# Token transposes as 64 rows by 64 columns on two row halves of TensorE's array, with other banks and an earlier place for the dt transposes

## The chip, the cores and the metric

One core of one Trainium2 chip runs the whole program. The metric is the device time of one execution in microseconds (us), the median of several runs. A profiled execution of the same program gives the trace.

## What is computed

Three steps on x (64 sequences of 32 tokens of 512 channels), all in float32. A conditional mixing of channels gives the input of a Mamba-2 block with 64 heads of 64 channels, 8 groups of 8 heads and a state of 128. Its output is added to x. Then a grouped convolution, a dense layer with a cluster mask, and a second addition.

```python
proj = jnp.einsum('bld,pd->blp', hidden_states, in_proj_w)
xBC  = silu(conv(proj[x, B, C]))            # 4 taps over the tokens
dt_p = softplus(dt + dt_bias);  dA = exp(dt_p * A)
dtx  = dt_p[..., None] * x                  # per token and head
state = state * dA_t + dtx_t * B_t;  y_t = state . C_t     # over 32 tokens
y = y + x * D
yn = y * rsqrt(mean(y*y per group) + eps) * norm_weight * silu(gate)
x = x + yn @ out_proj_w.T
x = x + masked(conv2(x) @ weight.T + bias)
```

## The kernel before

The Mamba part is 32 stages, `stage(n)`: a half of the tokens, one of the 8 groups of heads, and a block of 512 tokens (four tiles of 128). A stage has ten slots, m = 0 to 9. In slot m TensorE makes one 128 x 512 slice of the projection, `proj(n, m)` (line 487), as twelve matmuls in rounded float32: slots 0 and 1 are B and C, slots 2 to 5 the four slices of x, 6 to 9 those of the gate. The recurrence over 32 tokens is done as matrix products: G = B.C (`G_all`, line 621), the decays as exp of a product `seg` (lines 579 and 580) made by ScalarE (`expo`, line 588, tile Lt), M = decay times G on VectorE (`M_dve`, line 650, tile big), and `Y` (line 670), 64 by 64 products of dtx with M.

For dtx the slices of x, which lie with channels in the partitions, have to be turned so that tokens do. `A(n, i)` (line 610) does it for token tile i: four transposes of 128 x 128 with a 128 column identity as the moving operand, into one PSUM bank. Tiles 0 and 1 are turned at the end of slot 7, tiles 2 and 3 at the end of slot 9, right ahead of `Y(n, 0)` and `Y(n, 1)`. `A_dve` (line 641) multiplies a turned tile by dt out of PSUM. Tiles 2 and 3 are used in the next stage's slots 0 to 2, where `Y(n, 2)`, `Y(n, 3)` run. The output products `O(n - 1, i)` (line 770) of the stage before run in slots 1, 3, 4 and 5, each followed by its small sums `S` (line 738).

All five engines work in order, and the order is written out by hand: each `op` goes to its engine's queue where the Python code reaches it, each `wait` stops that engine alone until a named event. PSUM has eight banks: PP three for the projection in turn, PG for G and sums, PY two for Y, PO one for each output product, SEG two for the decays, and PT. TB lists the banks that the four token tiles are turned into: (PT, PO[2], PT, PO[0]). PO[0] is also SEG[0], so tile 3 waits until ScalarE has read the first decays, `L(n, 0)`; tile 2 waits for `dtx(n, 0)`, which frees PT.

Four times in the run a new block of dt values is made: `D_pe` (line 385) in slot 8 of stages 15, 16 and 0 (and at the start), then a chain of thirteen steps, `D_chain`, mostly on VectorE (lines 418 to 436, the last one `dsp` at line 427), of which the tuples `pace0` (stage 0) and `pace` (others) say how many are put ahead of each slot's work. `DT_pe` (line 444) turns the results, waiting for `dsp`; `DT_split` has ScalarE and VectorE copy them; `av` (line 560) has GpSimd make the operands of `seg` from the copies. In stages 0, 1, 16 and 17 (`turned_now`) these three stand in slot 6 behind `proj(n, 6)`; `seg(n)` follows in slot 8.

After stage 31 come `last_products` and the second part, which the change meets only through other bank numbers.

Of the kernel before, what the change touches and what calls it, by code (L numbers as in the profile page):

```python
# [56 lines left out]
def adaln_attn_ffn_kernel(nc, x, emb, gin, b2, wbank, biask, w_in, w_dt, w_out, prm, cst, cw4, ctxw,  # L57
                          w_ffn, b_ffn, asg, x2s, out):
    ctx = ExitStack()
    with ctx:  # L60
        def sb(name, shape, dt=F32):
            return ctx.enter_context(nc.sbuf_tensor(name, shape, dt))

        acc = sb("acc", [128, NT, XP])
        xh = sb("xh", [128, 4, 1024], FR)
        xl = sb("xl", [128, 4, 1024], FR)
# [15 lines left out]
        dtt = sb("dtt", [128, 8, 64])  # L82
# [6 lines left out]
        xs = big[:, 0:2048].rearrange("p (j t) -> p j t", j=4)  # L89
# [5 lines left out]
        dtx = sb("dtx", [128, 2, 512])  # L95
# [23 lines left out]
        pmx = gmt[:, 2, :]  # L119
        ex = gmt[:, 0:2, :]  # L120
        PS = ctx.enter_context(nc.psum_tensor("PS", [128, 8, 512], F32))
        PP, PT, PG, PY, PO = (0, 1, 4), 2, 3, (5, 6), (7, 7, 5, 6)
        SEG = (7, 6)
        TB = (PT, PO[2], PT, PO[0])

        book = {}
        pe, act, dve, pool, sp = (Queue(book) for _ in range(5))
        ident = C[:, C_ID:C_ID + 128]
# [4 lines left out]
        def bc(a, *shape):  # L133
            return a.to_broadcast(list(shape))
# [240 lines left out]
        def D_pe(b, free):  # L375
            a = 512 * (b % 2)
            pe.wait("wd", 0)
            pe.wait("wdl", 0)
            pe.wait("xl", 4 * b + 3)
            for w in free:  # L380
                pe.wait(*w)
            n = 0
            for k in range(4):
                for w, v in ((wdh, xh), (wdh, xl), (wdl, xh)):
                    fn = lambda e, k=k, w=w, v=v, n=n: e.matmul(PS[0:64, D_bank(b), :], w[:, 64 * k:64 * k + 64],
                                                                v[:, k, a:a + 512], start=(n == 0), stop=(n == 11))
                    pe.op(fn, "D", b) if n == 11 else pe.op(fn)
                    n += 1
# [50 lines left out]
        def DT_pe(b, free):  # L439
            pe.wait("dsp", b)  # L440
            for w in free:
                pe.wait(*w)
            for i, src in enumerate((dr[:, 0:128], dr[:, 128:256], da[:, 0:128], da[:, 128:256])):
                fn = lambda e, i=i, src=src: e.transpose(PS[:, SEG[0], 128 * i:128 * i + 128], src, ident)
                pe.op(fn, "DT", b) if i == 3 else pe.op(fn)

        def DT_split(b):
            a = 4 * (b % 2)
            turned = lambda t: t[:, a:a + 4, :].rearrange("p (r i) c -> p i r c", r=2)
            dt, av_ = (PS[:, SEG[0], k:k + 256].rearrange("p (i r c) -> p i r c", i=2, r=2) for k in (0, 256))  # L450
            act.wait("DT", b)
            act.op(lambda e: e.copy(turned(dtt), dt), "dtt", b)
            act.op(lambda e: e.copy(turned(ah), av_), "ah", b)
            dve.wait("ah", b)
            dve.op(lambda e: e.tensor_tensor(turned(al), av_, f(turned(ah)), ALU.subtract), "alo", b)
# [95 lines left out]
        def av(n):  # L551
            half, g, tb = who(n)
            b = 2 * half + tb
            pool.wait("dtt", b)
            pool.wait("ah", b)
            pool.wait("alo", b)
            if n >= 1:
                pool.wait("O", (n - 1, 3))
            for src, dst, kind in ((ah, avh, "avh"), (al, avl, "avl")):
                pool.op(lambda e, src=src, dst=dst: e.tensor_tensor(  # L560
                    dst.rearrange("p (i h t) -> p i h t", i=4, h=8),
                    bc(f(src[:, 4 * tb:4 * tb + 4, 8 * g:8 * g + 8]).rearrange("p i (h o) -> p i h o", o=1), 128, 4, 8, 32),
                    bc(C[:, C_V:C_V + 32].rearrange("p (a b t) -> p a b t", a=1, b=1), 128, 4, 8, 32), ALU.mult), kind, n)

        def seg(n):
            pe.wait("avh", n)
            pe.wait("avl", n)
            pe.wait("uf", 1)
            if n == 0:
                pe.wait("alo", 0)  # L570
            for r in range(2):
                if r == 0 and n - 1 in block_at:
                    pe.wait("ah", block_at[n - 1])
                    pe.wait("alo", block_at[n - 1])
                if n >= 1:
                    pe.wait("acc", (n - 1, 1 + 2 * r))
                else:
                    pe.wait("xl", 5 + r)
                pe.op(lambda e, r=r: e.matmul(PS[:, SEG[r], :], uf[:, :], avh[:, 512 * r:512 * r + 512], start=True, stop=False))
                pe.op(lambda e, r=r: e.matmul(PS[:, SEG[r], :], uf[:, :], avl[:, 512 * r:512 * r + 512], start=False, stop=True),  # L580
                      "seg", (n, r))
# [5 lines left out]
                    act.wait("M", (n - 1, 3))  # L587
                act.op(lambda e, r=r: e.activation(Lt[:, 512 * r:512 * r + 512], PS[:, SEG[r], :], ACT.Exp), "L", (n, r))  # L588

        def A(n, i):  # L590
            a = 128 * i
            if i == 2 and n in block_at:
                pe.wait("dre", (block_at[n], 1))
            if i == 0:
                if n == 0:
                    pe.wait("dre", (0, 1))
                elif n in block_at:
                    pe.wait("xl", 4 * block_at[n] + 3)
                for m in range(6):
                    pe.wait("silu", (n, m))  # L600
                if n >= 1:
                    pe.wait("dtx", (n - 1, 2))
            elif i == 1:
                pe.wait(*(("acc", (n - 1, 2)) if n >= 1 else ("xl", 7)))
            elif i == 2:
                pe.wait("dtx", (n, 0))
            else:
                pe.wait("L", (n, 0))
            for j in range(4):
                fn = lambda e, j=j: e.transpose(PS[:, TB[i], 128 * j:128 * j + 128], xs[:, j, a:a + 128], ident)  # L610
                pe.op(fn, "T", (n, i)) if j == 3 else pe.op(fn)

        def G_all(n):
            pe.wait("silu", (n, 0))
# [19 lines left out]
        def A_dve(n, i):  # L634
            half, g, tb = who(n)
            z, r = 4 * n + i, i % 2
            dve.wait("T", (n, i))
            dve.wait("dtt", 2 * half + tb)
            if z >= 2:
                dve.wait("Y", divmod(z - 2, 4))  # L640
            dve.op(lambda e: e.tensor_tensor(  # L641
                dtx[:, r, :].rearrange("p (h c) -> p h c", h=8), PS[:, TB[i], :].rearrange("p (h c) -> p h c", h=8),
                bc(dtt[:, 4 * tb + i, 8 * g:8 * g + 8].rearrange("p (h o) -> p h o", o=1), 128, 8, 64), ALU.mult), "dtx", (n, i))
        def M_dve(n, i):
            r = i % 2
            if i >= 2 or n >= 1:
# [85 lines left out]
        def S(n, tiles):  # L732
            last = (n, tiles[-1])
            pe.wait("ys2", last)
            pe.wait(*shared[0])
            shared[0] = ("var", last)
            for i in tiles:
                fn = lambda e, i=i: e.matmul(PS[:, PG, 256 + i:257 + i], yss[:, i, :], C[:, C_ONE:C_ONE + 1], start=True, stop=True)
                pe.op(fn, "S", last) if i == tiles[-1] else pe.op(fn)
# [72 lines left out]
        mixing_weights_pool(1)  # L812
        decay_rates()

        pace0 = (0, 3, 2, 3, 2, 3, 0, 0, 0, 3)
        pace = (0, 0, 0, 0, 5, 5, 0, 0, 0, 3)
        block_at = {0: 1, 15: 2, 16: 3}

        def X_tile(T, n):
# [7 lines left out]
        chain = []  # L827

        def stage(n):
            prev = n >= 1  # L830
            b = block_at.get(n)
            if n == 0:
                chain.extend(D_chain(0))
            for m in range(10):
# [31 lines left out]
                        add_out(n - 1, i)  # L866
                if m == 3 and not prev:
                    G_mask(n)
                turned_now = n == 0 or n - 1 in block_at
                if m == 6 and not turned_now:  # L870
                    av(n)
                if n == 0 and m == 6:
                    side_inputs()
# [13 lines left out]
                if m == 2:  # L887
                    silu(n, 1)
                evac(n, m)
                if m == 6 and turned_now:  # L890
                    t = block_at[n - 1] if n else 0
                    assert not chain
                    DT_pe(t, [("acc", (n - 1, 1)) if n else ("xl", 5)])
                    DT_split(t)
                    av(n)
                if n == 0 and m < 6:
                    split_w_hi(0, m + 4)
                    split_w_lo(0, m + 4)
# [32 lines left out]
                if prev:  # L931
                    for i in at("O"):
                        O(n - 1, i)
                        for tiles in sums(n - 1):
                            if tiles[-1] == i:
                                S(n - 1, tiles)
                if m == 7:
                    A(n, 0)
                    A(n, 1)
                if m == 8:  # L940
                    seg(n)
                    expo(n)
                    if b is not None:
                        D_pe(b, [("dtx", (n, 0))])
                        chain.extend(D_chain(b))
                if m == 9:
                    A(n, 2)
                    A(n, 3)
                    Y(n, 0)
                    Y(n, 1)  # L950

# [138 lines left out]

        FB = ((SEG[0], PP[2]), PY)

# [298 lines left out]
```

How the kernel before makes its waits and increments, by code:

```python
    def emit(self, eng, sems):  # L43
        seen = {}
        for it in self.items:
            if it[0] == "wait":
                v = self.book[it[1]][it[2]]
                if seen.get(it[1], 0) < v:
                    eng.wait_ge(sems[it[1]], v)
                    seen[it[1]] = v
            else:
                ins = it[1](eng)
                if it[2] is not None:
                    ins.then_inc(sems[it[2]], it[3])
```

## Time and profile before

| | |
|---|---|
| median of 3 runs | 1626.84 us (1625.94 to 1626.89) |
| the profiled execution | 1627.06 us, of which the span from first to last instruction 1625.3 us |
| TensorE matmuls busy | 1604.8 us, 99% of the span |
| weight loads | 1299.1 us, 80% |
| VectorE, ScalarE, GpSimd busy | 65%, 52%, 48% |
| mean granted TensorE clock | 0.998 |
| line 610 (token transposes) | 512 transposes, 272 ns each |

A matmul's time runs from its start until its last result is out, and the next one starts before that, so the busy time adds up to more than what an instruction costs the queue. What it costs is the distance from its start to the next one's start. In the timeline a row is a start, a duration over all merged instructions, an engine (PE is TensorE's matmuls, PEld its weight loads), a line, the tiles written and read (written<-moving,stationary in alphabetical order), the tile of the array (rows*columns), the moving operand's shape, and a count; in brackets is idle time before it and what ended it.

### The profile page before, as it was taken

What the parts mean: (1) busy time and instruction counts of PE and PEld (TensorE: products, weight loads), DVE (VectorE), ACT (ScalarE), POOL (GpSimd) and SP (SyncE); (2) the same over time, 40 slices, a digit from 0 to 9 for tenths busy, and PEclk for the clock granted to TensorE, in tenths of its full rate; (3) what the DMA queues carried; (4) which work ended last, traced back from release to release, by engine and by line L of the source; (5) the groups of instructions that cost most, each with busy time, mean ns of one, the idle gap of its engine ahead of it and who ended that gap; (6) DMA issues with size and microseconds to landing.
All of it is one profiled execution on the core that took longest, in us unless ns stands there. A gap on an engine that the chain in (4) does not pass through costs nothing. (4 is left out here: it accounts for less than half of the span.)

```text
span 1625.3 us, 31516 instructions
## 1 busy us (share of the span) xinstructions
PE 1604.8 (99%) x12495; PEld 1299.1 (80%) x12495; DVE 1059.1 (65%) x1741; ACT 845.9 (52%) x1372; POOL 773.4 (48%) x731
## 2 busy tenths in 40 slices
PE   9999999999999999999999999999999999999997
PEld 6778888888888888887787888888888888887665
DVE  6876666565656576676686656565667656565455
ACT  4654546555555545565554555555555556544321
POOL 3564644545453645454255554646364545534203
PEclk9999999999999999999999999999999999999999
DMA  5111102011111101011112201111110201116772
GB/s 190 59 53 33 41 20 66 27 53 40 40 53 34 59 16 58 21 53 40 33 41 73 65 28 53 41 40 53 34 59 8 66 21 53 41 36 153 181 156 104
DMA packets 50290, 93.08 MB, mean 57 GB/s; under 512 B 5664, under 2 KB 6304, under 8 KB 50144
## 3 DMA queue, kind: packets, MB, share of 16 engines
q1 hardware_dynamic: 50144, 91.06, 19.6%
q8 instruction: 100, 1.64, 0.4%
q14 instruction: 46, 0.38, 0.1%
HBM read 82.59 MB, written 8.45 MB: 56 GB/s over the span
## 5 line engine op out<-in xcount | busy, mean ns | idle before, releaser
L487 PE MATMUL PS<-xh,wh 128*128 128x512 f32 x1280 | 518.7, 405 | 0.6 <-DVE xl L369 0.6
L487 PE MATMUL PS<-xh,wl 128*128 128x512 f32 x1280 | 500.0, 391 | 0.0
L487 PE MATMUL PS<-xl,wh 128*128 128x512 f32 x1280 | 499.8, 390 | 0.0
L522 DVE SCALAR_TENSOR_TENSOR cb<-PS,P,cb 128x496 f32<-128x496 f32 (+2 forms) x576 | 412.6, 716 | 132.5 <-ACT cb L508 119.0
L184 POOL TENSOR_TENSOR wl<-rw,wh 128x512 fp32r<-128x512 f32 x160 | 211.8, 1328 | 188.6 <-ACT wh L179 170.6
L721 POOL TENSOR_TENSOR ysum<-yq 128x256 f32<-128x256 f32 x128 | 109.4, 855 | 364.0 <-ACT yq L706 363.8
L487 PEld LDWEIGHTS PS<-xh,wl 128*128 128x128 f32 x1280 | 240.2, 188 | 52.9
L487 PEld LDWEIGHTS PS<-xh,wh 128*128 128x128 f32 x1280 | 240.5, 188 | 49.1 <-ACT wh L179 1.0
L487 PEld LDWEIGHTS PS<-xl,wh 128*128 128x128 f32 x1280 | 241.0, 188 | 44.3
L508 ACT ACTIVATE cb<-PS,P 128x512 f32<-128x512 f32 x192 | 148.4, 773 | 205.2 <-PE PS L487 205.2
L650 DVE TENSOR_TENSOR big<-Lt,gmt 128x512 f32<-128x512 f32 x128 | 102.6, 843 | 158.0 <-ACT Lt L588 158.0
L770 PE MATMUL PS<-oh,yh 128*128 128x512 f32 x512 | 200.0, 391 | 2.4 <-POOL yl L730 2.4
L770 PE MATMUL PS<-ol,yh 128*128 128x512 f32 x512 | 199.2, 389 | 0.0
L770 PE MATMUL PS<-oh,yl 128*128 128x512 f32 x512 | 199.2, 389 | 0.0
L706 ACT ACTIVATE yq<-y 128x512 f32<-128x512 f32 x128 | 81.0, 633 | 207.0 <-DVE y L687 200.7
L512 ACT ACTIVATE big<-PS 128x512 f32<-128x512 f32 x128 | 76.2, 595 | 149.0 <-PE PS L487 148.7
L542 ACT ACTIVATE big<-cb 128x512 f32<-128x512 f32 x192 | 119.5, 623 | 62.7 <-DVE cb L522 62.5
L783 DVE SCALAR_TENSOR_TENSOR acc<-PS,rs,acc 128x512 f32<-128x512 f32 x128 | 93.1, 749 | 84.0 <-issue 45.9
L751 POOL TENSOR_TENSOR rs<-vr,mh 128x1 f32<-128x1 f32 (+1 forms) x95 | 57.0, 600 | 166.6 <-DVE vr L746 166.4
L641 DVE TENSOR_TENSOR dtx<-PS,dtt 128x512 f32<-128x512 f32 x128 | 82.1, 683 | 56.8 <-PE PS L610 56.8
L770 PEld LDWEIGHTS PS<-oh,yh 128*128 128x128 f32 x512 | 96.1, 188 | 23.0 <-issue 3.4
L770 PEld LDWEIGHTS PS<-oh,yl 128*128 128x128 f32 x512 | 96.1, 188 | 20.0
(197 smaller groups left out, 2230.6 us busy)
## 6 DMA issues: line engine op xcount, KB each, us to landing
rw<-in_w_in SPq DMA_DIRECT2D x160, 256.0 KB, 2.7
ro<-in_w_out SPq DMA_DIRECT2D x64, 256.0 KB, 2.9
wh<-x2s SPq DMA_DIRECT2D x32, 258.5 KB, 5.2
wl<-x2s SPq DMA_DIRECT2D x32, 258.5 KB, 5.1
x2s<-acc SPq DMA_DIRECT2D x16, 260.0 KB, 5.5
out_x<-acc SPq DMA_DIRECT2D x16, 256.0 KB, 2.3
acc<-in_x SPq DMA_DIRECT2D x3, 1024.0 KB, 9.4
acc<-in_x SPq DMA_DIRECT2D x4, 256.0 KB, 4.8
```

What stands on the lines that cost most here:

```text
L184: pool.op(lambda e: e.tensor_tensor(wl[:, m, :], rw[:, q % RW, :], f(wh[:, m, :]), ALU.subtract), "w_lo", (u, m))
L487: fn = lambda e, k=k, w=w, v=v, i=i: e.matmul(PS[:, bank, :], w[:, m, 128 * k:128 * k + 128], v[:, k, a:a + 512], start=(i == 0), stop=(i ...
L508: act.op(lambda e: e.activation(cb[:, z % 2, :], PS[:, bank, :], ACT.Identity, bias=P[:, P_CB + c:P_CB + c + 1], scale=P[:, P_CW + 4 * c + ...
L512: act.op(lambda e: e.activation(gate[:, m - 6, :], PS[:, bank, :], ACT.Silu), "ev", (n, m))
L522: dve.op(lambda e, d=d, w=w: e.scalar_tensor_tensor(out=cv[:, :, d:32], in0=pv[:, :, 0:32 - d], scalar=w, in1=cv[:, :, d:32], op0=ALU.mult ...
L542: act.op(lambda e: e.activation(dst, cb[:, z % 2, :], ACT.Silu), "silu", (n, m))
L641: dve.op(lambda e: e.tensor_tensor(dtx[:, r, :].rearrange("p (h c) -> p h c", h=8), PS[:, TB[i], :].rearrange("p (h c) -> p h c", h=8), bc ...
L650: dve.op(lambda e: e.tensor_tensor(Mb[:, r], bc(Lt[:, 256 * i:256 * i + 256].rearrange("p (h o t) -> p h o t", h=8, o=1), 128, 8, 2, 32), ...
L706: act.op(lambda e: e.activation(yq[:, :], y[:, r, :], ACT.Square), "yq", (n, i))
L721: pool.op(lambda e: e.tensor_tensor(ysum[:, :], yq[:, 0:256], yq[:, 256:512], ALU.add), "ys1", (n, i))
L770: fn = lambda e, j=j, v=v, w=w, q=q: e.matmul(PS[:, O_bank(n, i), :], v[:, r, 128 * j:128 * j + 128], w[:, j, :], start=(q == 0), stop=(q ...
L783: dve.op(lambda e: e.scalar_tensor_tensor(out=acc[:, T, 4:516], in0=PS[:, O_bank(n, i), :], scalar=rs[:, i:i + 1], in1=acc[:, T, 4:516], o ...
```

## The change

The token transposes become 64 by 64: `A(n, r)` now turns a pair of token tiles with sixteen instructions in place of eight. Each takes 64 partitions of xs (one row half, v = 0 or 1) with 128 token columns as the stationary operand and a 64 x 64 piece of the identity as the moving one, and writes 64 columns into the bank of its half. The pair of tiles shares the two banks. `A_dve` reads its tile out of both banks, and waits for the pair's one event. Banks are renumbered so that each pair is adjacent: PP (0, 1, 2), PT 6, PY (4, 5), PO (7, 7, 5, 4), SEG (7, 4). The waits move with it: the first pair waits for `dtx(n - 1, 3)` and `acc(n - 1, 2)` at its start, the second for `dtx(n, 1)` and `L(n, 0)` at its start. `D_pe` waits for `dtx(n, 1)`. In stages 1, 16 and 17 `DT_pe` and `DT_split` move from behind `proj(n, 6)` to the end of slot 5, behind `O(n - 1, 3)` and its sums; `av` goes to the head of slot 6. The chain's pace changes from 5 and 5 steps in slots 4 and 5 to 7 and 3, in stage 0 from 3, 2, 3, 2, 3 in slots 1 to 5 to 3, 3, 3, 3, 1.

```diff
-        PP, PT, PG, PY, PO = (0, 1, 4), 2, 3, (5, 6), (7, 7, 5, 6)
-        SEG = (7, 6)
-        TB = (PT, PO[2], PT, PO[0])
+        PP, PT, PG, PY, PO = (0, 1, 2), 6, 3, (4, 5), (7, 7, 5, 4)
+        SEG = (7, 4)
+        TB = ((PO[2], PT), (PT, PO[0]))
...
-                    pe.wait("xl", 5 + r)
+                    pe.wait("xl", 5 + 2 * r)
...
-        def A(n, i):
...
-            for j in range(4):
-                fn = lambda e, j=j: e.transpose(PS[:, TB[i], 128 * j:128 * j + 128], xs[:, j, a:a + 128], ident)
-                pe.op(fn, "T", (n, i)) if j == 3 else pe.op(fn)
+        def A(n, r):
+            if r == 0:
+                for m in range(6):
+                    pe.wait("silu", (n, m))
+                if n == 0:
+                    pe.wait("dre", (0, 1))
+                    pe.wait("xl", 7)
+                else:
+                    pe.wait("dtx", (n - 1, 3))
+                    pe.wait("acc", (n - 1, 2))
+                if n in block_at and n >= 1:
+                    pe.wait("xl", 4 * block_at[n] + 3)
             else:
+                pe.wait("dtx", (n, 1))
                 pe.wait("L", (n, 0))
+                if n in block_at:
+                    pe.wait("dre", (block_at[n], 1))
+            for i in (0, 1):
+                a = 128 * (2 * r + i)
+                for j in range(4):
+                    for v in (0, 1):
+                        p, c = slice(64 * v, 64 * v + 64), 256 * i + 64 * j
+                        fn = lambda e, j=j, v=v, a=a, p=p, c=c: e.transpose(PS[:, TB[r][v], c:c + 64], xs[p, j, a:a + 128],
+                                                                         ident[p, 64 * v:64 * v + 64])
+                        pe.op(fn, "T", (n, 2 * r + 1)) if (i, j, v) == (1, 3, 1) else pe.op(fn)
...
+            b0 = TB[i // 2][0]
+            dve.wait("T", (n, i | 1))
...
+                dtx[:, r, :].rearrange("p (j v c) -> p j v c", j=4, v=2),
+                PS[:, b0:b0 + 2, 256 * r:256 * r + 256].rearrange("p v (j c) -> p j v c", j=4),
...
-        pace0 = (0, 3, 2, 3, 2, 3, 0, 0, 0, 3)
-        pace = (0, 0, 0, 0, 5, 5, 0, 0, 0, 3)
+        pace0 = (0, 3, 3, 3, 3, 1, 0, 0, 0, 3)
+        pace = (0, 0, 0, 0, 7, 3, 0, 0, 0, 3)
...
-                turned_now = n == 0 or n - 1 in block_at
-                if m == 6 and not turned_now:
+                if n >= 1 and m == 6:
                     av(n)
...
-                if m == 6 and turned_now:
-                    t = block_at[n - 1] if n else 0
+                if n == 0 and m == 6:
                     assert not chain
-                    DT_pe(t, [("acc", (n - 1, 1)) if n else ("xl", 5)])
-                    DT_split(t)
-                    av(n)
+                    DT_pe(0, [("xl", 5)])
+                    DT_split(0)
+                    av(0)
...
+                if n - 1 in block_at and m == 5:
+                    assert not chain
+                    DT_pe(block_at[n - 1], [("acc", (n - 1, 1))])
+                    DT_split(block_at[n - 1])
                 if m == 7:
                     A(n, 0)
-                    A(n, 1)
...
-                        D_pe(b, [("dtx", (n, 0))])
+                        D_pe(b, [("dtx", (n, 1))])
...
                 if m == 9:
-                    A(n, 2)
-                    A(n, 3)
+                    A(n, 1)
```

## Rows read from the trace of the kernel before

**Rows 1.** The page, part 1: busy time, share of the span, instructions.
```profile
PE 1604.8 (99%) x12495; PEld 1299.1 (80%) x12495; DVE 1059.1 (65%) x1741; ACT 845.9 (52%) x1372; POOL 773.4 (48%) x731
```

**Rows 2.** Timeline of TensorE, stage 15, first group of transposes (start, us, engine, ...).
```profile
747.62 1.03 PE L610 MATMUL PS<-C,big 128*128 128x128 f32 x8
748.41 0.48 PE L487 MATMUL PS<-xh,wh 128*128 128x512 f32 x1
748.72 0.39 PE L487 MATMUL PS<-xl,wh 128*128 128x512 f32 x1
748.95 0.40 PE L487 MATMUL PS<-xh,wl 128*128 128x512 f32 x1
```

**Rows 3.** TensorE's groups by shape (busy us, mean ns), then durations min/median/max by line.
```profile
L610 PEld LDWEIGHTS PS<-C,big 128*128 128x128 f32 x512 | 59.7, 140 | 8.3
L738 PEld LDWEIGHTS PS<-C,big 128*128 128x128 f32 x256 | 43.0, 189 | 7.4
...
L610 PE MATMUL PS<-C,big x512: 270/272/273, 58.6 to 1491.2; 128*128 128x128 f32 x171
...
L670 PE MATMUL PS<-big,dtx x4096: 218/218/268, 71.5 to 1500.0; 64*64 64x64 f32 x196
```

**Rows 4.** Timeline of TensorE, stage 15: from 128 rows to 64, and one Y.
```profile
716.14 0.39 PE L487 MATMUL PS<-xh,wl 128*128 128x512 f32 x1
716.46 0.49 PE L355 MATMUL PS<-ab,xb 64*128 64x512 f32 x1
...
718.21 1.16 PE L670 MATMUL PS<-big,dtx 64*64 64x64 f32 x64
719.30 0.46 PE L621 MATMUL PS<-big 128*32 128x32 f32 x32
```

**Rows 5.** Timeline of TensorE, stage 14, second group, Y, next projection.
```profile
702.81 1.03 PE L610 MATMUL PS<-C,big 128*128 128x128 f32 x8
703.88 1.30 PE L670 MATMUL PS<-big,dtx 64*64 64x64 f32 x64
705.11 0.50 PE L487 MATMUL PS<-xh,wh 128*128 128x512 f32 x1
705.45 0.40 PE L487 MATMUL PS<-xl,wh 128*128 128x512 f32 x1
```

**Rows 6.** Timeline of ScalarE and VectorE beside rows 5; what line 670 waited for.
```profile
699.37 0.60 ACT L512 ACTIVATE big<-PS 128x512 f32<-128x512 f32 x1 [1.68 <-PE PS L487]
...
702.51 1.09 ACT L588 ACTIVATE Lt<-PS 128x512 f32<-128x512 f32 x2
...
703.13 1.29 DVE L650 TENSOR_TENSOR big<-Lt,gmt 128x512 f32<-128x512 f32 x2 [4.20 <-ACT Lt L588]
...
  DVE big L650: 6.1, 26
```

**Rows 7.** Timeline of VectorE and TensorE in stage 0, around the second group.
```profile
67.55 1.29 DVE L650 TENSOR_TENSOR big<-Lt,gmt 128x512 f32<-128x512 f32 x2 [3.10 <-ACT Lt L588]
...
70.52 1.03 PE L610 MATMUL PS<-C,big 128*128 128x128 f32 x8
```

**Rows 8.** Timeline of TensorE and VectorE in stage 17, the dt transposes.
```profile
844.75 0.48 PE L487 MATMUL PS<-xh,wh 128*128 128x512 f32 x1
...
848.12 0.44 PE L444 MATMUL PS<-C,dr 128*128 128x128 f32 x2 [0.37 <-DVE da L427]
...
856.47 0.47 PE L579 MATMUL PS<-yh,uf 128*128 128x512 f32 x1 [1.34 <-issue]
...
836.26 1.35 DVE L430 TENSOR_TENSOR da<-pb,dr 128x256 f32<-128x256 f32 x1
```

**Rows 9.** Timeline of TensorE in stage 1, the same place.
```profile
102.53 0.48 PE L487 MATMUL PS<-xh,wh 128*128 128x512 f32 x1
...
105.89 0.44 PE L444 MATMUL PS<-C,dr 128*128 128x128 f32 x2 [0.38 <-DVE da L427]
...
113.97 0.47 PE L579 MATMUL PS<-yh,uf 128*128 128x512 f32 x1 [1.05 <-issue]
```

More of the change, by code:

```diff
@@ L588, in expo @@
                 act.op(lambda e, r=r: e.activation(Lt[:, 512 * r:512 * r + 512], PS[:, SEG[r], :], ACT.Exp), "L", (n, r))
-        def A(n, i):
[L591 to L594, printed above, removed]
+        def A(n, r):
+            if r == 0:
+                for m in range(6):
+                    pe.wait("silu", (n, m))
                 if n == 0:
                     pe.wait("dre", (0, 1))
-                elif n in block_at:
-                    pe.wait("xl", 4 * block_at[n] + 3)
[L599 to L606, printed above, removed]
+                    pe.wait("xl", 7)
[3 more added lines that the diff above has]
+                if n in block_at and n >= 1:
+                    pe.wait("xl", 4 * block_at[n] + 3)
             else:
+                pe.wait("dtx", (n, 1))
                 pe.wait("L", (n, 0))
-            for j in range(4):
-                fn = lambda e, j=j: e.transpose(PS[:, TB[i], 128 * j:128 * j + 128], xs[:, j, a:a + 128], ident)
-                pe.op(fn, "T", (n, i)) if j == 3 else pe.op(fn)
+                if n in block_at:
[8 more added lines that the diff above has]
+                        pe.op(fn, "T", (n, 2 * r + 1)) if (i, j, v) == (1, 3, 1) else pe.op(fn)
         def G_all(n):
@@ L636, in A_dve @@
             z, r = 4 * n + i, i % 2
-            dve.wait("T", (n, i))
+            b0 = TB[i // 2][0]
+            dve.wait("T", (n, i | 1))
             dve.wait("dtt", 2 * half + tb)
@@ L641, in A_dve @@
             dve.op(lambda e: e.tensor_tensor(
-                dtx[:, r, :].rearrange("p (h c) -> p h c", h=8), PS[:, TB[i], :].rearrange("p (h c) -> p h c", h=8),
-                bc(dtt[:, 4 * tb + i, 8 * g:8 * g + 8].rearrange("p (h o) -> p h o", o=1), 128, 8, 64), ALU.mult), "dtx", (n, i))
+                dtx[:, r, :].rearrange("p (j v c) -> p j v c", j=4, v=2),
+                PS[:, b0:b0 + 2, 256 * r:256 * r + 256].rearrange("p v (j c) -> p j v c", j=4),
+                bc(dtt[:, 4 * tb + i, 8 * g:8 * g + 8].rearrange("p (j v o) -> p j v o", j=4, v=2), 128, 4, 2, 64), ALU.mult), "dtx", (n, i))
         def M_dve(n, i):
```

## The prediction

> **What bounds the kernel now.** I read the page first, then TensorE's own timeline stage by stage, and only then the other engines at the places where TensorE stood still. The page has TensorE's matmuls busy 99% of the span [rows 1], and no other engine above 65%. So the time is the sum of the distances from one matmul's start to the next one's, and a change on another engine counts only where TensorE waits for it. Outside such waits the timeline is very regular: a 128x512 matmul is followed by the next after 0.23 us (the last two rows of [rows 2]), and the distances repeat from stage to stage. Every cost below is such a distance. The reader should look at the starts, not at the durations.
>
> Two places matter. In slot 7 the first group of eight transposes stands between two projections, and nothing waits: it costs 0.79 us (747.62 to 748.41), and the projection behind it comes up to speed late, 0.31 us to its second matmul in place of 0.23 [rows 2], about 0.11 us with what follows. So the first group costs 0.90 us. In slot 9 the second group stands ahead of Y. There the starts are 702.81 and 703.88 [rows 5], but I don't read that as the price of the transposes, because Y also waits for M: ScalarE's two exps start at 702.51 and take 1.09, so the first ends near 703.1; VectorE starts the first M at 703.13, two take 1.29 [rows 6], so the first M ends near 703.8, and Y starts just after it. Line 670 is released by M 26 times [rows 6].
>
> **The price of a new transpose.** The eight old ones start 0.109 us apart (a round). Why decides what halving brings. A token transpose has a weight load of 140 ns; another float32 load of 128 columns takes 189 [rows 3]. So the transposes' load is some 50 ns shorter, and the load alone doesn't fill 109 ns. The matmul with 128 moving columns takes 272 ns, that of Y with 64 takes 218 [rows 3]: 54 ns for 64 columns, 108 for 128. That is the round: the moving columns bound it and the load hides behind them. With 64 moving columns it is 54, and the load of 128 columns (109 less 50, some 58) about equals it. So a row half does one transpose per 58 ns or so, if the load stays as short.
>
> Whether both halves work at once is shown by Y alone. One Y pair is 64 instructions on four 64*64 tiles with one bank for each row half, the same split. It takes 1.09 us to the next line [rows 4] = 16 rounds of four. Taking 0.11 for the first round (load, then columns) and 0.15 for the drain before the next tile shape, the other fourteen rounds come to 0.83/14 = 0.059 us. Row halves and column halves run together there. I take 0.059 for a round of two new transposes; the other end is 0.059 for each transpose alone, and 0.11 a round if the load turns long.
>
> **The price of the switch.** Rows 4 show the same tile shape, 64*128, entered from the projection: 716.14 to 716.46 is 0.32 us in place of 0.23, so 0.09 for the drain. Leaving 64 rows costs more: the last round drains (0.15), and the next projection needs 0.34 us to its second matmul (705.11 to 705.45 [rows 5]), 0.11 over the usual and some 0.02 more behind it. Old transposes had no entry and little exit cost, as they have the projection's own shape. The Trainium skill, TensorEngine Tiling, section Key Properties, says that changing the tiling mode drains TensorE; the rows above agree and give its size.
>
> **First group, 32 stages.** New: entry 0.09, first round 0.11, six rounds of 0.059 = 0.35, the drain 0.15 and a few ns for the second half, exit 0.13: 0.84 us. Old 0.90. So 0.06 a stage, 32 times = 1.9 us saved. The transposes themselves fall from 0.87 to 0.46; the two switches take nearly all of it back. All of what follows on the other engines moves along: ScalarE idles 1.68 us until the projection of slot 8 is done (699.37 [rows 6]), so it is driven by TensorE here and gives the gain through.
>
> **Second group, 27 ordinary stages.** The chain that sets Y's start runs from the end of projection 8 over ScalarE (silu, skip product, weight split, table load, exps) to the first M, and doesn't contain the transposes. It stays. The new group waits for the first L at its start (near 703.1, 0.3 us after TensorE gets there), then takes 0.11 + 0.35 + 0.15 = 0.61: done near 703.77, some 0.1 ahead of Y's old start at 703.88. Zero gained, zero lost, with M as the cover; were that cover gone, the gain would be 0.26 a stage. The second half of Y waits for the second M (Y takes 1.23 here, 1.09 where M is early [rows 4, 5]), so an earlier start would bring nothing either.
>
> **Second group, stages with M early.** In stage 0 both M are done by 68.84 and the group starts at 70.52 [rows 7]. There the old group costs 8 x 0.109 + 0.1 = 0.97 to Y, the new one 0.09 + 0.61 = 0.70. Stages 0, 15, 16 (a dt product stands behind seg) and 31 are such: 4 x 0.26 = 1.0 us saved.
>
> **dt transposes, stages 1 and 17.** Moving them ahead of projection 6 pays only if the chain's last step is done by then. In stage 17 TensorE gets to projection 6 at 844.75. The dt transposes ran at 848.12, released by line 427, the chain's end [rows 8], after a stall of 0.5 behind the projection (whose twelve matmuls fill 2.83). In the new order TensorE stands at the wait from 844.75: 3.3 us with nothing to do, and projection 6 is behind it. The new pace moves two steps from slot 5 to slot 4, ahead of the taps there; but VectorE works without idling from 836.26 [rows 8] to slot 5, so its total ahead of the last step is the same, and I move that end by at most 0.2. What goes is the old stall 0.5 and the wait of seg for av on GpSimd (1.34 before 856.47 by the profile, 1.5 as distance): seg now comes after the work of GpSimd. Net 3.3 - 2.0 = 1.3 later. Stage 1 in the same way: 102.53 to 105.89, 3.3 us; gone are 0.5 and 1.2 (1.05 before 113.97) [rows 9]: 1.6 later. With the stall gone before seg, these two become ordinary and Y waits for M again: 0.14 each. In stage 16 the chain ends before TensorE reaches even the new place: 0. In stage 0 the place stays, VectorE is full ahead of it, and the reshuffled pace brings 0 (bounds -0.5 and +0.5). Sum +3.2 us. The bounds for the two stages are 0 stall left (then both stalls go: -3.7) and 1 us more each.
>
> **The rest at nothing.** Bank numbers change no instruction. `A_dve` reads two banks with the same 512 elements; Y's reader on VectorE has that pattern already, and dtx is needed three slots later. `dtx(n, 0)` may start up to 0.4 us later, with over 5 us until slot 9. The new waits of `A(n, 0)` are for events two slots old. `D_pe` waits for dtx(n, 1), done long before.
>
> **Sum.** -1.9 - 1.0 + 3.2 = +0.3 us on the profiled 1627.06; that execution is 0.2 above the median, so 1626.84 + 0.3 = 1627.1 us.
>
> **The rivals.** (1) The chain ends in time: VectorE gets through the seven steps while it would otherwise wait for slot 4's data, and the stalls of stages 1 and 17 vanish. Then -3.7 in place of +3.2 (with up to half of it more likely than all): 1620 to 1624. For it: seven steps are put where the taps wait for ScalarE. Against: rows 8 show no such idle time. (2) The switch is cheaper for the transposes than for line 355 and Y, as both are in float32 and leave no long column stream: drains nearly vanish, first group 0.55, so 32 x 0.3 = 10 more: 1617. Against: rows 4 and 5. The Trainium skill, TensorEngine Tiling, section Theoretical Speedup, gives up to 2x for 64 rows; for both groups that would be half of 64 x 0.87, 28 us, which the wait for M in slot 9 alone rules out. (3) Slower by a long load: with 64 rows the transposes' load loses its short form and takes 109 ns like the others of 128 columns. A round stays at 0.11, sixteen instructions do the old work, and the switches come on top. First group 0.09 + 0.94 + 0.13 = 1.16, +0.26 x 32 = 8.3; second group past M's time by 0.2 to 0.25, of which Y's own wait gives 0.14 back, +0.08 x 27 = 2.2, and 0.3 for the others; with dt +3.2: +14, 1641. It decides from a round of about 0.07 on. The Trainium skill, TensorE: Matmul & The Clock Gate, section LDWEIGHTS, has the load go by its columns alone, 107 ns for 128: by that rule this rival would hold; the 140 against 189 ns in rows 3 speak against it. (4) The halves take turns: 16 x 0.059, first group 1.29, +12; second group +6.5; with dt +22: 1649. Against it: Y's rounds. (5) My drains are off by 0.05: inside the forecast's own range.
>
> **Chances.** The forecast (within 1624 to 1630) 0.50; rival 1 0.16; rival 2 0.06; rival 3 0.10; rival 4 0.06; other slower ways, as the second group ending behind M by 0.1 to 0.2 us, 0.12 (1630 to 1635). The range takes in rival 1 and rival 3 and leaves out 2 and 4: 1620 to 1641. A measurement of this kernel tells 0.2%, 3.3 us, from no change. Faster 0.22, same 0.50, slower 0.28. The forecast's own range is 1624 to 1630.
>
> **What would show it.** Right: in slot 7 the group and what follows at 0.7 and 0.1 us, rounds of 59 ns, weight loads of 140 ns, 0.32 us entry; in slot 9 Y still released by line 650 with Y's start 1.0 to 1.1 after the end of projection 9; idle time of some 3 us before line 444's successor in stages 1 and 17 and none before line 579 there. Wrong: loads of 188 ns (rival 3), starts 59 ns apart one by one (rival 4), no stall before the dt transposes (rival 1), a next projection that starts within 0.1 us of the last transpose (rival 2).

## The result, and the profile after

The changed kernel takes 1629.66 us (median of 20 runs, 1627.28 to 1631.98) against 1626.87 us of the kernel before, run beside it. The ratio is 1.0015, interval 1.0009 to 1.0022: 2.8 us more. That is a small slowdown clear of noise, inside the 0.2% that was taken as no change (the interval ends just above it). The profiled execution took 1628.14 us, its span 1626.4 us, only 1.1 us over the span before. That gap between the profile and the median is a finding of its own, below.

The page, part 1 (busy us, share of the span, instructions), and what TensorE waited for (us in total, times, longest), of the changed kernel:

```profile
PE 1595.7 (98%) x13007; PEld 1278.0 (79%) x13007; DVE 1056.9 (65%) x1741; ACT 845.3 (52%) x1372; POOL 774.1 (48%) x731
...
PE PS L444 <- DVE da L427: 6.7, 3, 3.2
PE PS L612 <- ACT Lt L588: 6.5, 28, 0.3
PE PS L775 <- POOL yl L735: 2.4, 2, 1.5
...
PE PS L579 <- issue: 1.7, 1, 1.7
```

TensorE is 9 us less busy than in [rows 1], and waits more: 6.7 us for the end of the dt chain, and 28 times for the first exp (line 588) at the head of the second group. Of the waits before `seg` (line 579) only that of stage 0 is left. In the kernel before, the same two waits were:

```profile
PE PS L579 <- issue: 4.1, 3, 1.7
...
PE PS L444 <- DVE da L427: 1.6, 3, 0.8
```

The first group of transposes, now line 612, timeline of TensorE in stage 13, and the line's durations (min/median/max):

```profile
650.28 0.39 PE L487 MATMUL PS<-xh,wl 128*128 128x512 f32 x1
650.60 0.71 PE L612 MATMUL PS<-C,big 64*128 64x64 f32 x16
651.25 0.50 PE L487 MATMUL PS<-xh,wh 128*128 128x512 f32 x1
651.58 0.39 PE L487 MATMUL PS<-xl,wh 128*128 128x512 f32 x1
...
L612 PEld LDWEIGHTS PS<-C,big x1024: 134/139/143, 57.9 to 1492.2; 64*128 64x128 f32 x171
L612 PE MATMUL PS<-C,big x1024: 221/222/278, 57.9 to 1492.3; 64*128 64x64 f32 x171
```

Entry 0.32 us in place of 0.23, sixteen transposes and the drain 0.64 (640 to 644 ns in each of the 32 stages, where the old eight took 790), then 0.33 to the second matmul of the projection. With 0.02 to 0.03 behind it that is 0.09 + 0.64 + 0.13 = 0.86, against 0.90 in [rows 2]. The load still takes 139 ns and the matmul has fallen by 50 to 222; the reading of [rows 3] was 54.

The second group in stage 13, all engines (compare [rows 5, 6]):

```profile
657.33 1.09 ACT L588 ACTIVATE Lt<-PS 128x512 f32<-128x512 f32 x2
...
657.95 1.29 DVE L655 TENSOR_TENSOR big<-Lt,gmt 128x512 f32<-128x512 f32 x2 [5.31 <-ACT Lt L588]
658.04 0.61 PEld L612 LDWEIGHTS PS<-C,big 64*128 64x128 f32 x16 [0.57 <-issue]
658.07 0.71 PE L612 MATMUL PS<-C,big 64*128 64x64 f32 x16 [0.18 <-ACT Lt L588]
...
658.71 1.29 PE L675 MATMUL PS<-big,dtx 64*64 64x64 f32 x64
...
659.93 0.19 PEld L487 LDWEIGHTS PS<-xh,wh 128*128 128x128 f32 x1
```

The transposes stand and wait for the exp, and Y follows 0.64 us after their start, when both the group and the first M (which ends near 658.65) are through. Those 0.64 us are what the first group takes, where nothing is waited for: so in 28 stages the transposes now stand in the chain themselves, between the exp and Y, and end when M does. From the start of the exps to Y it is 1.38 us, and it was 1.37 in [rows 5, 6] (702.51 to 703.88). Y's start came out 0.01 us later and Y itself 0.01 shorter. Nothing came back here.

The dt transposes in stages 1 and 17, TensorE's timeline, and the granted clock (PEclk, 1.00 is 2.4 GHz) of two stretches:

```profile
101.35 0.28 PE L743 MATMUL PS<-C,big 128*128 128x1 f32 x2
104.83 0.44 PE L444 MATMUL PS<-C,dr 128*128 128x128 f32 x2 [3.21 <-DVE da L427]
...
110.87 0.71 PE L612 MATMUL PS<-C,big 64*128 64x64 f32 x16
...
843.80 0.28 PE L743 MATMUL PS<-C,big 128*128 128x1 f32 x2
847.26 0.69 PE L444 MATMUL PS<-C,dr 128*128 128x128 f32 x2 [3.19 <-DVE da L427]
...
849.03 0.63 PE L487 MATMUL PS<-xh,wl 128*128 128x512 f32 x1
849.46 0.63 PE L487 MATMUL PS<-xh,wh 128*128 128x512 f32 x1
...
854.83 0.71 PE L612 MATMUL PS<-C,big 64*128 64x64 f32 x16
...
104.00:106.00 2.00, 1.17 (x7) 1.06 (x8) 1.93 (x4) 0.48 (x2) 0.00 (x0) 1.00 0.44 131
846.00:850.00 4.00, 2.74 (x9) 2.35 (x10) 3.52 (x8) 0.65 (x2) 0.20 (x2) 0.63 0.25 70
...
848.00:850.00 2.00, 2.00 (x7) 1.61 (x6) 1.70 (x4) 0.65 (x2) 0.19 (x1) 0.50 0.06 23
```

Both stalls are 3.2 us. Behind the one in stage 17 the matmuls start 0.43 us apart in place of 0.23 and last 0.63 in place of 0.39: the granted clock, the third figure from the right, is 0.50 there, its lower level, 1.2 GHz (0.63 is the mean of a stretch with both levels). From the dt transposes to the first group it is 6.04 us in stage 1 (104.83 to 110.87) and 7.57 in stage 17 (847.26 to 854.83): the lower clock costs 1.5 us. In this execution it happened once. Of the 20 timed runs, the four with a mean granted clock of 0.998 took 1627.3 to 1628.2 us, the two with 0.993 took 1631.7 and 1632.0, most of the others were at 0.996 and near 1629.7. That fits the median's 1.5 us over the profiled execution, if most executions lose the 1.5 us once more than this one; only this one has a trace, so that isn't shown. The Trainium skill, TensorE: Matmul & The Clock Gate, section What's actually happening, says that the clock gate takes the array to half rate when it has been idle. The rows of stage 17 agree, behind a stall of 3.2 us; in stage 1 the clock stayed up behind a stall as long.

### The profile page after: what moved, and what is told of

The parts are those of the page before. It is cut to its first block and busy times, and to the rows that moved or that the text cites. A ratio compares the mean times of both kernels' runs of the same rounds, so it can differ in the third digit from the quotient of the medians.

```text
span 1626.4 us, 32575 instructions
## 1 busy us (share of the span) xinstructions
PE 1595.7 (98%) x13007; PEld 1278.0 (79%) x13007; DVE 1056.9 (65%) x1741; ACT 845.3 (52%) x1372; POOL 774.1 (48%) x731
```

## The experiments

My theory after the comparison: the new transposes save what was forecast, the dt part loses more than that by its stalls, and by the clock behind them. The first four runs test this.

**The transposes alone.** The changed kernel with the dt part as before:

```diff
-        pace0 = (0, 3, 3, 3, 3, 1, 0, 0, 0, 3)
-        pace = (0, 0, 0, 0, 7, 3, 0, 0, 0, 3)
+        pace0 = (0, 3, 2, 3, 2, 3, 0, 0, 0, 3)
+        pace = (0, 0, 0, 0, 5, 5, 0, 0, 0, 3)
...
+                if m == 6 and turned_now:
+                    t = block_at[n - 1] if n else 0
                     assert not chain
...
+                    DT_pe(t, [("acc", (n - 1, 1)) if n else ("xl", 5)])
+                    DT_split(t)
+                    av(n)
...
-                if n - 1 in block_at and m == 5:
-                    assert not chain
-                    DT_pe(block_at[n - 1], [("acc", (n - 1, 1))])
-                    DT_split(block_at[n - 1])
```

> The changed kernel with the dt transposes back behind projection 6 and the old pace: the new transposes and banks alone. Theory (the parts add up, and the added time is the dt part): the first groups save 0.045 us in each of 32 stages, the second groups 0.3 us in stages 0, 15, 16 and 31, nothing in the others: 2.5 us under the kernel before, 1624.2 us, with its two short stalls before the dt transposes and a granted clock of 0.998 in all runs. Rival (the half arrays are what lowers the granted clock): the clock is 0.996 in most runs here too and the time 1626 us or more.

Measured: 1624.29 us (11 runs) against 1627.07, ratio 0.9978 (0.9970 to 0.9987), granted clock 0.997 to 0.999 in every run. The rival about the clock is out: with sixteen half-array transposes in all 64 groups the mean stays where it was. The saving is 2.8 us, where 2.5 were expected here and 2.9 in the prediction.

**The dt part alone.** The kernel before with `DT_pe` and `DT_split` at the end of slot 5 and the new pace tuples, the reverse of the diff above.

> The kernel before with the dt transposes at the end of slot 5 and the new pace, old transposes and banks. Theory: stalls of 3.2 to 3.5 us in stages 1 and 17 in place of the old 1.7 and 2.0, and a granted clock at its lower level behind one or both of them: 1631 to 1632.5 us, granted clock 0.996 or less in most runs. Rival (the dt part costs only the difference of the stalls, the rest is the transposes'): 1628.5 to 1629.5 us at 0.998.

Measured: 1632.18 us (5 runs), ratio 1.0032 (1.0019 to 1.0044), 5.1 us slower, granted clock 0.993 to 0.996. Its profiled execution has the same stalls, and the lower clock behind both; the windows (granted clock is the third figure from the right) show it:

```profile
PE PS L444 <- DVE da L427: 6.8, 3, 3.2
...
102.00:112.00 10.00, 6.86 (x25) 5.62 (x26) 5.82 (x11) 3.01 (x8) 5.79 (x5) 0.83 0.10 27
844.00:854.00 10.00, 6.81 (x27) 5.57 (x26) 8.10 (x16) 2.57 (x5) 3.09 (x4) 0.83 0.15 47
```

The two parts add up: -2.8 + 5.1 = +2.3, and the whole change measured +2.8.

**TensorE kept busy while it waits.** The changed kernel with matmuls whose result nobody reads, in stages 1 and 17:

```diff
+                if n in (1, 17) and m == 5:
+                    pe.wait("dtx", (n - 1, 3))
+                    pe.wait("w_hi", (n // 2, 9))
+                    for _ in range(14):
+                        pe.op(lambda e: e.matmul(PS[:, PT, :], wh[:, 9, 0:128], xh[:, 0, 512:1024], start=True, stop=True))
                 if n - 1 in block_at and m == 5:
```

> The changed kernel with 14 idle matmuls of 128x512 (3.2 us, into the free bank PT, their result unused) ahead of the dt transposes in stages 1 and 17, so that TensorE is busy while it waits. Theory (the stall lowers the granted clock for the matmuls behind it): the wait ends at the same time, the clock stays at its upper level, 0.998 in all runs, and the median falls from 1629.7 to 1626.5 to 1627.5 us. Rival (the lower clock comes from something else): 0.996 and 1629.7 us as before, or slower by what the matmuls take beyond the wait.

Measured: 1626.82 us (11 runs), 2.8 us under the changed kernel with 28 more matmuls and no less to wait for; ratio to the kernel before 0.9997 (0.9988 to 1.0006). Its timeline in stage 17 and the same two windows:

```profile
844.01 3.45 PE L944 MATMUL PS<-xh,wh 128*128 128x512 f32 x14
847.38 0.44 PE L444 MATMUL PS<-C,dr 128*128 128x128 f32 x2
...
102.00:112.00 10.00, 10.00 (x59) 7.84 (x59) 6.17 (x12) 4.56 (x10) 5.87 (x5) 1.00 0.08 27
844.00:854.00 10.00, 10.00 (x61) 7.93 (x59) 5.87 (x11) 4.58 (x10) 5.78 (x5) 1.00 0.08 28
```

The dt transposes run at nearly the same place in time (847.38, and 847.26 in the changed kernel), and the clock stays at 1.00. The wait is no shorter, only filled; so the idle time, and not the wait, is what the lower clock follows. Against the transposes alone (1624.29, measured beside it) this kernel takes 2.5 us more: that is what the dt part costs at the upper level. Of its 5.1 us the other 2.6 to 2.8 are the lower clock.

Of the 11 runs three still show a mean of 0.996, and so do some of the kernel before, which has no such stall. The traces show one other place. In stage 0 TensorE waits for a silu at line 624 (621 in the kernel before), 0.2 us in some executions and 1.4 to 3.4 in others. Behind a long one the clock was at its lower level in four of five traces, here in that of the transposes alone:

```profile
36.63 0.55 PE L624 MATMUL PS<-big 128*32 128x32 f32 x32 [1.51 <-ACT big L542]
...
37.70 0.63 PE L487 MATMUL PS<-xl,wh 128*128 128x512 f32 x1
```

So a mean of 0.996 alone doesn't tell where the clock fell. What speaks for the dt stalls is the count: 16 of 20 runs of the changed kernel lie at 0.997 or less, 3 of 11 with the stalls filled.

**What hides the second group.** As the transposes alone, and `seg` and the exps of slot 8 stand ahead of ScalarE's skip product and weight splits:

```diff
                 evac(n, m)
+                if m == 8:
+                    seg(n)
+                    expo(n)
...
                 if m == 8:
-                    seg(n)
-                    expo(n)
                     if b is not None:
```

> As t_only, and ScalarE does the two exps of slot 8 straight behind the gate's silu, ahead of the skip product and the weight splits. Theory (in the 27 ordinary stages Y is released by the chain exp, M and not by the transposes): the first exp ends about 1.2 us earlier, the second group is followed by Y 0.64 us after its start and Y takes 1.09 in place of 1.22: 0.4 us in each of 27 to 29 stages, 11 us under t_only, about 1613 us. Rival (the group of slot 9 is bounded by its own drains, or ScalarE gives the time back later in the stage): within 2 us of t_only.

Measured: 1614.47 us (5 runs), ratio 0.9921 (0.9908 to 0.9933), 9.8 us under the transposes alone. Stage 13 again:

```profile
652.63 1.09 ACT L588 ACTIVATE Lt<-PS 128x512 f32<-128x512 f32 x2
653.26 1.29 DVE L655 TENSOR_TENSOR big<-Lt,gmt 128x512 f32<-128x512 f32 x2 [4.19 <-ACT Lt L588]
...
654.24 0.71 PE L612 MATMUL PS<-C,big 64*128 64x64 f32 x16
...
654.88 1.02 PEld L675 LDWEIGHTS PS<-big,dtx 64*64 64x64 f32 x64
654.88 1.16 PE L675 MATMUL PS<-big,dtx 64*64 64x64 f32 x64
```

Both M end at 654.55, before Y's 654.88; no row of a wait is left. The second group is now bounded by its own transposes.

**The same order in the kernel before.** The last diff on the kernel before, with its old transposes.

> The kernel before with the exps of slot 8 straight behind the gate's silu, old transposes, old dt place. Theory (the wait for M hides the second group's transposes, old and new): with M early the old group still needs 0.97 us to Y, so only the 0.10 us of the even stages and the 0.135 us inside Y come back, 5 us: 1622 us. The new transposes with the same order (1614.5) then stand 7.5 us below it, against 2.7 us without: the difference is what M hid. Rival (the earlier exps bring their gain by themselves, whatever the transposes): 1616 us or less, as far below the kernel before as the other was below its own.

Measured: 1621.86 us (6 runs), ratio 0.9966 (0.9954 to 0.9978), 5.2 us faster. Stage 13 with the old transposes:

```profile
655.32 1.29 DVE L650 TENSOR_TENSOR big<-Lt,gmt 128x512 f32<-128x512 f32 x2 [4.44 <-ACT Lt L588]
...
656.22 1.03 PE L610 MATMUL PS<-C,big 128*128 128x128 f32 x8
657.18 1.16 PE L670 MATMUL PS<-big,dtx 64*64 64x64 f32 x64
```

Both M end at 656.61, and Y starts 0.96 us after the group, against 0.64 with the new one. The new one's entry takes 0.09 of the difference back, so some 0.24 us a stage is what halving gives here. So the new transposes are worth 7.4 us where the exps come first (1621.86 against 1614.47) and 2.8 us where they don't. The 4.6 us between are what the wait for the exp and M hid.

**Four of one half, then four of the other.** As the transposes alone:

```diff
-                for j in range(4):
-                    for v in (0, 1):
+                for v in (0, 1):
+                    for j in range(4):
```

> As t_only (new transposes, old dt place), but four transposes of one row half and then four of the other, in place of taking turns. Theory (the halves run at once only when they take turns): starts 59 ns apart within a run of four, the group lasts 0.91 us to the next line in place of 0.64; 0.27 us in each first group, and 0.14 us net in each second one: 12 to 14 us over t_only, 1636 to 1638 us. Rival (weight loads or matmuls of one half overlap as well as those of two): group at 0.64 to 0.70 us, 1624 to 1627 us.

Measured: 1626.21 us (10 runs), 1.9 us over the transposes alone, not 12 to 14. The group of stage 13:

```profile
650.00 0.77 PE L612 MATMUL PS<-C,big 64*128 64x64 f32 x16
650.69 0.50 PE L487 MATMUL PS<-xh,wh 128*128 128x512 f32 x1
```

0.69 us, 0.05 over the alternating order: one round more, not eight. My expectation fell: the halves don't need to take turns one by one. Read one at a time, the starts of the group are 0, 14, 112, 125, 175, 186, 236 and 250 ns and so on: still in pairs. Those of one half alone start 62 ns apart (the next run), so a pair must be one of each half: transposes of the second half start before some of the first that stand ahead of them in the queue. How deep that reaches was not tried.

**One half alone.** As the transposes alone, but v runs over (0,) only. The other half of each turned tile isn't made, so the work is half and the result is not used as a value.

> As t_only, with the transposes of the lower row half alone (v = 0): eight in place of sixteen in a group, the other half of the turned values is left out. Theory (the halves run at once, so the second half's transposes cost 4 ns each group): the group still lasts 0.63 to 0.64 us to the next line and the time is that of t_only, 1624.0 to 1624.4 us. Rival (each transpose takes a place of its own in the queue, and a round of two is longer than a round of one): 0.05 us or more less in each group, 1622.5 us or less.

Measured: 1624.77 us (10 runs), against 1624.29 with both halves (other series of runs; the intervals of the two ratios overlap). The group lasts as long (649.76 to 650.40) with eight as with sixteen:

```profile
649.76 0.71 PE L612 MATMUL PS<-C,big 64*128 64x64 f32 x8
650.40 0.50 PE L487 MATMUL PS<-xh,wh 128*128 128x512 f32 x1
```

So the second half's transposes are free to within some 4 ns a group, and what a row half costs is its own eight rounds and the two switches.

**The chain earlier.** The changed kernel with the ten steps ahead of slots 1 to 4:

```diff
-        pace = (0, 0, 0, 0, 7, 3, 0, 0, 0, 3)
+        pace = (0, 1, 2, 3, 4, 0, 0, 0, 0, 3)
```

> The changed kernel with the chain's ten steps of stages 1, 16 and 17 ahead of slots 1 to 4 (1, 2, 3, 4) in place of 4 and 5 (7, 3). Theory (the dt part is slower only because the chain ends 3.3 us after TensorE gets to its wait): the chain ends ahead of that, no stall before the dt transposes and none before seg, no lower clock: 1620 to 1622 us, granted clock 0.998. Rival (VectorE is full in slots 1 to 4, and the steps make taps or y late, so TensorE waits elsewhere for as long): 1626 us or more.

Measured: 1627.44 us (11 runs), ratio to the kernel before 1.0004 (0.9995 to 1.0013): 2.2 us under the changed kernel, where 8 to 10 were expected. Stage 1, TensorE and VectorE, and TensorE's waits:

```profile
103.79 0.35 PE L743 MATMUL PS<-C,big 128*128 128x1 f32 x2
105.43 0.41 PE L444 MATMUL PS<-C,dr 128*128 128x128 f32 x2 [1.29 <-DVE acc L788]
...
101.08 0.35 DVE L427 TENSOR_SCALAR da<-dr,scol 128x256 f32<-128x256 f32 x1
...
104.53 1.41 DVE L788 SCALAR_TENSOR_TENSOR acc<-PS,rs,acc 128x512 f32<-128x512 f32 x2 [0.90 <-POOL rs L756]
...
PE PS L624 <- ACT big L542: 3.5, 2, 3.4
PE PS L444 <- DVE acc L788: 2.6, 2, 1.3
...
PE PS L355 <- DVE xl L369: 1.6, 2, 1.4
PE PS L775 <- ACT yh L719: 1.4, 2, 0.7
```

The chain does end in time (101.43, TensorE arrives at 103.9). But the second thing that the dt transposes wait for, `acc(n - 1, 1)`, which frees their bank, comes at 105.3; and two waits are new: for y at an output product (0.7 us, line 775, in stages 1 and 17) and for the split at a mixing product (1.4 us, line 355, in stage 16). The rival held in part: the stall shrank from 3.2 to 1.3 + 0.7 us a stage. And 1627.44 is no better than the 1626.82 of the kernel whose stalls are only filled, so what was gained can be the clock alone. The longest wait of the list, 3.4 us at line 624, is the one of stage 0 that comes and goes from execution to execution; the median doesn't rest on this trace.

What bounds `acc(n - 1, 1)` is in part VectorE's work ahead of it: the taps, which the steps have pushed back, end at 103.57. But then VectorE stands 0.90 us until GpSimd has made rs. Another order, with the sums' steps ahead of the taps, was not tried, so this stall isn't shown to be the least possible.

**All together.** The chain earlier, with the exps of slot 8 first:

> As chain_early, and with the exps of slot 8 first as in t_exp_first: everything together. Theory: 4 us below t_exp_first's 1614.5 for the stalls that are gone (0.5 and 1.2 in stage 1, 0.5 and 1.5 in stage 17), so about 1610.5 us. Rival (the earlier steps collide with the y work of slots 0 to 3): 1614 us or more.

Measured: 1615.58 us (5 runs), ratio 0.9931 (0.9919 to 0.9944), 1.1 us over the kernel with the dt transposes behind projection 6. The rival held: the 4 us below 1614.5 didn't come. Which of the two places is better the runs don't tell, as they overlap (1615.0 to 1617.5 and 1612.8 to 1616.0).

**The new pace with the old place.** The transposes, the exps first, the dt transposes behind projection 6, and the pace tuples of the change:

> As t_exp_first (new transposes, exps first, dt transposes behind projection 6), with the changed kernel's pace tuples. Theory (of the new pace only stage 0 gains, as its chain ends earlier there; in stages 1, 16 and 17 the chain ends at the same time): 0.5 to 0.7 us below t_exp_first, 1613.8 to 1614.0 us. Rival (the stall in stage 0 before seg is set by GpSimd and takes the gain back): 1614.5 us.

Measured: 1613.21 us (4 runs), ratio to the kernel before 0.9918 (0.9903 to 0.9933), 13.7 us faster than it. Against 1614.47 the 1.3 us have runs that overlap (1612.8 to 1614.4 and 1612.8 to 1616.0), and 0.5 to 0.7 were expected, so a gain of the pace is not shown. In the profile of the changed kernel the wait of stage 0 before the dt transposes is 0.33 us in place of 0.81. Its median is the lowest of the study.

## Why the prediction was right, and where it was not

The sum said 1627.1 us, the measurement 1629.66, both within 0.2% of the kernel before. The measured time is inside the forecast's own range, 1624 to 1630, by 0.3 us. The parts were right in kind, but the sum had +0.3 us of change where 2.8 were measured, and nearly all of those are a term that it didn't have, the clock. That the time still fell inside is owed to the width of the range, and in part luck: the two runs at 0.993 took 1631.7 and 1632.0. Step by step:

- *Price of a transpose.* 0.059 us for a round of two, by moving columns and with a short load: the load is 139 ns, the matmul 222, the group to its successor 0.64 against 0.61 in the sum (8 rounds of about 0.062, where I had 0.059). Half the transposes take the same time. Rivals 3 and 4 are out.
- *Switch.* Entry 0.09 and exit 0.13, as summed. The two switches take back most of the 0.4 us. Rival 2 is out. First group: 0.04 us a stage saved in place of 0.06, 1.3 us in place of 1.9.
- *Second group, ordinary stages.* Nothing gained and nothing lost, right (28 stages, not 27). Its cover was thinner than said: I had the group end 0.1 us ahead of Y's old start (703.77; from 703.1 and 0.61 it would be 703.71, the figure holds 0.05 more that the text doesn't name), but it starts 0.15 us after the exp's end and lasts 0.64. It is done when M is. What to see there was put as "Y still released by line 650"; in fact the wait moved to the head of the transposes, for line 588 (28 times). The price of that cover is shown: 9.8 us come free when the exps go first. The prediction's 0.26 a stage is 0.24 where M is early; it lacked the 0.13 inside Y.
- *Stages with M early.* The transposes alone saved 2.8 us, the sum had 2.9. The agreement is partly chance: the first groups gave 0.6 less, and with the dt transposes at their old place stages 1 and 17 have M early too, six stages of 0.24 in place of four.
- *Dt transposes.* The stall of 3.3 us is 3.2 in both stages, the waits before `seg` are gone in these two, and the pace left the chain's end where it was. VectorE does idle ahead of that end, 0.9 us for GpSimd's rs, before and after the change; the prediction had it without idling, which changed nothing here. A term is missing: the dt part costs 5.1 us and not 3.2, because TensorE ran at 1.2 GHz behind one or both of the stalls, 1.5 us each time that it happened. I costed the stall by its length alone, though the sum had made a gap in TensorE longer than any in its ordinary stages. At the upper level the part costs 2.5, less than summed; the 0.5 of stage 0 is most of that difference. The clock's 2.6 to 2.8 us are the 2.5 by which the sum is low.
- *Stage 0.* I had 0; the chain ends 0.5 us earlier. Bounds held.

Rival 1, the chain in time, is refuted as it stands in the change, and the run with the chain earlier shows that even then another wait (the bank of `acc(n - 1, 1)`) takes its place.

## What to carry to other kernels

Before costing a faster group of matmuls, look at what its successor waits for: here half of the transposes stood under a wait for exp and M, and moving two calls, `seg` and `expo`, was worth more (5.2 us) than halving the transposes (2.8), and both together more than their sum (12.6). A step moved ahead of filler work turns the filler into a stall if its input isn't ready; cost that stall by its length and by the clock behind it. Tile switches of TensorE had a price here (0.22 us and a drain), so short groups gained little by a half array.

## What the runs showed of the hardware

- Two row halves with a bank each run transposes at once: sixteen last as long as eight (0.64 us), and four in a row in one half, then four in the other, cost only 0.05 us more a group (0.69).
- A float32 transpose's weight load of 128 columns is 139 ns, against 189 for other float32 loads of 128 columns. With 64 moving columns the transposes of a row half start 62 ns apart; whether load or columns set that was not separated.
- After an idle stretch of 3.2 us TensorE's matmuls ran at 1.2 GHz in some cases and not in others: in one execution in stage 17 and not in stage 1, in another (the dt part alone) in both. A wait of 1.5 us in stage 0 was followed by it once, too. Matmuls without use in the gap kept 2.4 GHz and made the kernel 2.8 us faster.
